# Carried-state products of an mLSTM block: fp32 products on 32 rows, against fp16 halves stacked over 128 partitions by the DMA queue

## The reference

```python
def step(carry, xs):                       # for every token of a sequence
    C, n, m = carry
    q_t, k_t, v_t, i_t, f_t = xs
    f_log = jax.nn.log_sigmoid(f_t)
    m_new = jnp.maximum(f_log + m, i_t)
    F = jnp.exp(f_log + m - m_new)
    I = jnp.exp(i_t - m_new)
    C_new = F[..., None, None] * C + (I[..., None] * k_t)[..., :, None] * v_t[..., None, :]
    n_new = F[..., None] * n + I[..., None] * k_t
    h_num = jnp.einsum('bhd,bhdv->bhv', q_t * scale, C_new)
    qn = jnp.einsum('bhd,bhd->bh', q_t * scale, n_new)
    h = h_num / (jnp.maximum(jnp.abs(qn), jnp.exp(-m_new)) + EPS)[..., None]
...
x = x + (sigmoid(o_preact) * multihead_norm(h)) @ Wout.T
x = x + gelu(layernorm(x) @ w1_q.T + b1) @ w2_q.T + b2
```

## Time and profile before

| | |
|---|---|
| median of 3 runs | 1802.92 us |
| the profiled execution | 1805.18 us |
| its span | 1803.4 us |
| TensorE busy (matmul) | 1755.5 us, 97% |
| VectorE busy | 1373.7 us, 76% |
| ScalarE busy | 1069.4 us, 59% |
| GpSimd busy | 588.0 us, 33% |
| mean granted TensorE clock | 0.983 of 2.4 GHz |

### The profile page before, as it was taken

One profiled execution on the slowest core, in us unless ns is written; L12 is line 12 of the kernel. 1 busy time (PEld: TensorE's weight loads), 2 busy tenths in 40 slices (PEclk: granted clock), 3 DMA queues, 4 the chain that ended last, 5 costly groups with the idle time before them and its releaser, 6 DMA issues.

```text
span 1803.4 us, 31974 instructions
## 1 busy us (share of the span) xinstructions
PE 1755.5 (97%) x12524; PEld 882.3 (49%) x12524; DVE 1373.7 (76%) x2464; ACT 1069.4 (59%) x1801; POOL 588.0 (33%) x481
## 2 busy tenths in 40 slices
PE   5779999999999999999999999999999999999999
PEld 3464544445454444544445454444544444454555
DVE  6777777788777778878777787877778777885772
ACT  5866638375573737547374764737466383756643
POOL 1232342514324251432524143252423325242340
PEclk8859999999999999999999999999999999999999
DMA  8423225151422524142251413325142332414020
GB/s 287 173 83 103 54 69 128 48 150 23 122 54 53 144 48 140 23 127 58 54 144 38 132 41 106 80 54 144 36 114 49 98 100 54 121 25 127 1 53 24
DMA packets 233526, 156.97 MB, mean 87 GB/s; under 512 B 195089, under 2 KB 199313, under 8 KB 228257
## 3 DMA queue, kind: packets, MB, share of 16 engines
q1 hardware_dynamic: 231792, 151.79, 31.0%
q10 hardware_dynamic: 1584, 3.15, 0.5%
HBM read 90.48 MB, written 17.24 MB: 60 GB/s over the span
## 4 chain that ended last, share of the span: by engine, by line
PE 91%; DVE 2%; ACT 1%; issue 1%; POOL 1%; DMA 0%; POOLq 0%; DVEq 0%; ACTq 0%
PE pf L1976 24%; PE pf L1960 23%; PE pa L1819 20%; PE pa L1795 9%; PE psh L1819 6%; PE psh L1916 2%; PE psh L1900 1%; PE psh L1877 1%; PE pa L1786 1%; PE psh L1950 1%; PE psh L1858 1%; PE pa L1916 1%; PE psh L1833 1%; DVE kT L1468 0%; ACT dec L930 0%
## 5 line engine op out<-in xcount | busy, mean ns | idle before, releaser
L1976 PE MATMUL pf<-w2T,gT 128*128 128x512 f16 x2048 | 497.1, 379 | 0.0
L1960 PE MATMUL pf<-x2T,w1T 128*128 128x512 f16 x1920 | 422.1, 380 | 0.0
L1960 PEld LDWEIGHTS pf<-x2T,w1T 128*128 128x128 f16 x1920 | 185.3, 98 | 222.7
L1522 DVE SCALAR_TENSOR_TENSOR gT<-g,wscale,gT 128x512 f16<-128x512 f32 x240 | 212.2, 884 | 105.7 <-ACT gT L966 105.1
L1976 PEld LDWEIGHTS pf<-w2T,gT 128*128 128x128 f16 x2048 | 195.3, 97 | 176.4
L1819 PE MATMUL pa<-wT,xT 128*128 128x512 f16 x960 | 213.6, 380 | 1.0 <-ACT sig L889 0.9
L963 ACT ACTIVATE g<-pf,b1c 128x512 f32<-128x512 f32 x240 | 164.0, 683 | 75.7 <-PE pf L1960 73.5
L971 ACT ACTIVATE ktok<-kT 128x512 f32<-128x512 f32 x64 | 40.4, 631 | 265.0 <-DVE kT L1446 265.0
L1819 PE MATMUL pa<-wT,shared 128*128 128x512 f16 x768 | 177.7, 382 | 0.7 <-DMA shared<-qT 0.6
L966 ACT ACTIVATE gT<-g,wscale 128x512 f16<-128x512 f32 x240 | 173.2, 722 | 7.8
L1795 PE MATMUL pa<-xT,wT 128*128 128x512 f16 x768 | 171.3, 380 | 0.1
(11 more groups left out here) (228 smaller groups left out, 2679.6 us busy)
## 6 DMA issues: line engine op xcount, KB each, us to landing
dec<-gate_r SPq DMA_DIRECT2D x32, 1024.0 KB, 5.6
xin<-L_attn_x SPq DMA_DIRECT2D x16, 1024.0 KB, 6.1
out<-x1b SPq DMA_DIRECT2D x64, 256.0 KB, 2.2
xres<-L_attn_x SPq DMA_DIRECT2D x16, 512.0 KB, 5.9
xres<-L_attn_x SPq DMA_DIRECT2D x32, 256.0 KB, 3.0
qw<-gate_w SPq DMA_DIRECT2D x128, 48.0 KB, 5.7
gT<-L_ffn_w SPq DMA_DIRECT2D x5, 1024.0 KB, 4.8
gT<-L_ffn_w ACTq DMA_DIRECT2D x3, 1024.0 KB, 5.9
```

What stands on the lines that cost most here:

```text
L1522: nc.vector.scalar_tensor_tensor(gT[:, LO, f, :], g32[:, f % 2, :], wscale[:, W_GELU:W_GELU + 1], gT[:, HI, f, :], ALU.mult, ALU.subtract) ...
L1960: last = nc.tensor.matmul(bank, w1T[:, k, tok(f)], x2T[:, part, :, k, :], start=(k == 0 and part == HI), stop=(k == KD - 1 and part == LO))
L1976: last = nc.tensor.matmul(bank, gT[:, part, f, tok(t)], w2T[:, f, :], start=(f == 0 and part == HI), stop=(f == NF - 1 and part == LO), sk ...
```

## The change

The product with the state is taken in f16 halves. The four products of halves, HI HI, HI LO, LO HI and LO LO, are 4 x 32 = 128 rows of one product. VectorE makes the halves of `qw` and `cst` (`split_queries`, `split_states`, two instructions each), SP copies them with 32 small DMAs into stacked form (`stack_states`), and `chunk_head` issues one f16 product of 128 rows in front of each head's three. Sequence 0 stays as it was. The halves lie in `kT` (queries) and `ktok` (states), so `head_stats(b, 0)` on VectorE waits for all 32 DMAs before it writes there. The constants (SCORE_SPLIT, ONES, Q_STACK and the scales made from them) change values only.

```diff
+        s4 = sb("s4", [P, H4, T - 1, HG, VA], F16)
+        q4_first = sb("q4_first", [P, HG, LATE], F16)
...
+        q4 = [q4_first[:, :, :], qw_half[:, 0, :, :], qw_half[:, 1, :, :],
+              xres[:, T - 1, :].bitcast(F16)[:, 0:HG * LATE].rearrange("p (g s) -> p g s", g=HG)]
...
+            def stack_states(b):
+
+                sp.wait_ge(q16_ok, at(b - 1, 1, 1))
+                for i in range(H4):
+                    for r in range(4):
+                        sp.dma_start(q4[i][r * DQ:(r + 1) * DQ, :, :],
+                                     q16[i * DQ:(i + 1) * DQ, r // 2, :, :]).then_inc(q4_loaded, 16)
+                sp.wait_ge(s16_ok, at(b - 1, 1, 1))
+                for i in range(H4):
+                    for r in range(4):
+                        sp.dma_start(s4[r * DQ:(r + 1) * DQ, i, :, :, :].rearrange("p c g v -> p (c g v)"),
+                                     s16[i * DQ:(i + 1) * DQ, r % 2, :]).then_inc(s4_loaded, 16)
...
                 transpose_x(b + 1)
+                stack_states(b)
                 heads_out(b, b - 1)
...
+            def split_queries(b):
+
+                dve.wait_ge(qw_ok, at(b, 1, 1))
+                nc.vector.tensor_scalar(q16[:, HI, :, :], qw[:, :, :], split_scale[:, 2:3], None, ALU.mult).then_inc(q16_hi, 1)
+                dve.wait_ge(q16_hi, at(b - 1, 1, 1))
+                nc.vector.scalar_tensor_tensor(q16[:, LO, :, :], qw[:, :, :], split_scale[:, 2:3], q16[:, HI, :, :],
+                                               ALU.mult, ALU.subtract).then_inc(q16_ok, 1)
+
+            def split_states(b):
+
+                states = cst[:, :, :, :].rearrange("p c g v -> p (c g v)")
+                dve.wait_ge(ph_free, at(b, PH_USES, U_U + 1))
+                nc.vector.tensor_scalar(s16[:, HI, :], states, split_scale[:, 3:4], None, ALU.mult).then_inc(s16_hi, 1)
+                dve.wait_ge(s16_hi, at(b - 1, 1, 1))
+                nc.vector.scalar_tensor_tensor(s16[:, LO, :], states, split_scale[:, 3:4], s16[:, HI, :],
+                                               ALU.mult, ALU.subtract).then_inc(s16_ok, 1)
...
+                if j == 0 and not (isinstance(b, int) and b == 0):
+                    dve.wait_ge(q4_loaded, at(b - 1, 256, 256))
+                    dve.wait_ge(s4_loaded, at(b - 1, 256, 256))
                 den_of = den[:, :].rearrange("p (a h) -> p a h", h=H4)
...
                     hidden(0, 1)
+                    split_queries(b)
...
                         state(b, 2)
+                        if run_f:
+                            split_states(b)
...
-                if j == 1:
+                if j == 1 and not (isinstance(b, int) and b == 0):
+                    pe.wait_ge(q4_loaded, at(b - 1, 256, 256))
+                    pe.wait_ge(s4_loaded, at(b - 1, 256, 256))
+                elif j == 1:
                     pe.wait_ge(qw_ok, at(b, 1, 1))
...
+                    if j > 0:
+                        nc.tensor.matmul(out_cols, q4[i][:, g, tok(j - 1)], s4[:, i, j - 1, g, :], start=(j == 1 and g == 0),
+                                         stop=False, skip_group_check=True)
```

More of the change, by code:

```diff
@@ L39 @@
 V_SPLIT = 2.0 ** -5 / X_SCALE
-SCORE_SPLIT = 2.0 ** -16
+SCORE_SPLIT = 2.0 ** -20
+ONES = 2.0 ** 10
+Q_STACK = 2.0 ** 27
 TINY = 2.0 ** -100
@@ L144, in block_program @@
         gcol = sb("gcol", [P, KD])
-        split_scale, head_scale = sb("split_scale", [P, 2]), sb("head_scale", [P, 3])
+        split_scale, head_scale = sb("split_scale", [P, 4]), sb("head_scale", [P, 3])
         evac = sb("evac", [P, 6])
@@ L186, in block_program @@
         square = head_sum[:, :, 0:DHV]
+        q16 = (kT[:, :, :].bitcast(F16).rearrange("p g s -> p (g s)")[:, 0:2 * HG * LATE]
+               .rearrange("p (a g s) -> p a g s", a=2, g=HG))
+        s16 = (ktok[:, :, :].bitcast(F16).rearrange("p c d -> p (c d)")[:, 0:2 * HG * (T - 1) * VA]
+               .rearrange("p (a n) -> p a n", a=2))
+        qw_half = qw[:, :, :].bitcast(F16).rearrange("p g s -> p (g s)").rearrange("p (i g s) -> p i g s", i=2, g=HG)
+        q4 = [q4_first[:, :, :], qw_half[:, 0, :, :], qw_half[:, 1, :, :],
+              xres[:, T - 1, :].bitcast(F16)[:, 0:HG * LATE].rearrange("p (g s) -> p g s", g=HG)]
         k_halves, q_halves = (hoT[:, :, :, :, :].rearrange("p t a k c -> p (t a k c)")
@@ L261, in block_program @@
         cst_ok = sem("cst_ok")
+        q16_hi, q16_ok, s16_hi, s16_ok = sem("q16_hi"), sem("q16_ok"), sem("s16_hi"), sem("s16_ok")
+        q4_loaded, s4_loaded = sem("q4_loaded"), sem("s4_loaded")
         kq_split = sem("kq_split")
@@ L568, in _ @@
             residual(B - 1, RES_TILES[1])
+            stack_states(B - 1)
             heads_out(B - 1, B - 2)
@@ L587, in _ @@
             nc.gpsimd.memset(half[:, :], -0.5)
-            nc.gpsimd.memset(vaug[:, :, :, DHV:VA], 1.0).then_inc(s_pchain, 1)
+            nc.gpsimd.memset(vaug[:, :, :, DHV:VA], ONES).then_inc(s_pchain, 1)
             pool.wait_ge(s_pchain, 1)
@@ L1152, in scales @@
                     nc.vector.tensor_scalar(gate_bias[:, :], gate_bias[:, :], 1.0 / CAP, None, ALU.mult)
-                    nc.vector.tensor_scalar(head_scale[:, 2:3], wscale[:, W_V:W_V + 1], MLSTM_EPS * 2.0 ** -10,
+                    nc.vector.tensor_scalar(head_scale[:, 2:3], wscale[:, W_V:W_V + 1], MLSTM_EPS * 2.0 ** -10 / ONES ** 2,
                                             wscale[:, W_V:W_V + 1], ALU.mult, ALU.mult)
@@ L1162, in scales @@
                     nc.vector.tensor_scalar(evac[:, W_GELU:W_GELU + 1], to_score, score * DQ ** -0.5 / X_SCALE, None, ALU.mult)
-                    nc.vector.tensor_scalar(head_scale[:, 0:1], to_score, score, to_score, ALU.mult, ALU.mult)
-                    nc.vector.tensor_scalar(head_scale[:, 1:2], to_score, MLSTM_EPS * score, to_score, ALU.mult, ALU.mult)
+                    nc.vector.tensor_scalar(head_scale[:, 0:1], to_score, score * ONES, to_score, ALU.mult, ALU.mult)
+                    nc.vector.tensor_scalar(head_scale[:, 1:2], to_score, MLSTM_EPS * score * ONES, to_score, ALU.mult, ALU.mult)
                     nc.vector.tensor_scalar(evac[:, W_O:W_O + 1], winv[:, W_O:W_O + 1], 1.0 / X_SCALE, None, ALU.mult)
@@ L1169, in scales @@
                     nc.vector.tensor_scalar(split_scale[:, 1:2], qk, 2.0 ** -5 / score, None, ALU.mult)
+                    nc.vector.tensor_scalar(split_scale[:, 2:3], qk, Q_STACK, None, ALU.mult)
+                    nc.vector.tensor_scalar(split_scale[:, 3:4], wscale[:, W_QK:W_QK + 1], 1.0 / Q_STACK, None, ALU.mult)
                     nc.vector.tensor_scalar(gcol[:, :], gcol[:, :], wscale[:, W_OUT:W_OUT + 1], None, ALU.mult).then_inc(s_scales, 1)
```

## The result

The changed kernel takes 1866.99 us (median of 4 runs, 1865.49 to 1869.24), beside 1802.76 us for the kernel before on the same chip. The ratio is 1.0352 (95% interval 1.034 to 1.0364): 64 us slower. The spans of the two profiled executions are 1864.2 and 1803.4 us, 60.8 apart. The forecast was slower, by 19 us, with a range that ended at 1843.

The account below looks back on a forecast made before the run. PE, busy 97% of the span, was taken to bound the kernel. Chunk 3, waiting on VectorE's delayed chain, cost 0.9 us a block and the second scores 0.37: 1.25, 19 us in all, so 1803.4 became 1822, range 1795 to 1843.

Parts of the forecast that it names:

- the 0.84 us of gain: PE's stream per block: 1.60 us of state products removed, less 0.76 for 24 new short products; 12.6 us in all.
- the stall at the scores: PE waits for banks before the second group's scores, since VectorE's query split delays the weighs: 0.37 us a block (0 to 0.8).
- the forecast chain: Late state copies hold VectorE's head_stats(0) from 318.79 to 322.3, so PE's chunk 3 starts at 336.75, not 336.11.
- Their pace: eight loads of 32 partitions take SP 3.67 us, 0.46 each: SP's 16 state copies, issued from 313.9 at 0.46 us each: the last issued at 320.8, landed at 322.2.
- the forecast's own sum: Per block: project(0) 0.9 us later behind VectorE's chain, plus 0.37 at the second scores: 1.25 us, 19 us in all.
- PE at chunk 1 wants them at 322.66 - no loss yet: State copies land at 322.2, before PE's chunk 1 needs them at 322.66, so PE loses nothing there.
- rival C: SBUF-to-SBUF copies land after 5.7 us, like the qw loads: 65 us more, 1887; chance 0.06, shared with anything above 1845.
- The chain's inner lengths: VectorE in head_stats: 6.5 us from start to the copy of chunk 1's sums, then 7.25 to chunk 2's.
- Rival A: Faster, copies come in time, at a pace of 0.33 us: 1796, or 1790 without the wait before the second scores; chance 0.21.

## Why the prediction was half right

**What held.** PE's side: the new products cost 2.71 us for 8 heads against 2.48, 0.029 us each (forecast 0.0315), so the 0.84 us of gain is real; the kernel without copies shows it, less the stall at the scores. The states' halves were ready 1.59 us after the start of `state(2)` (315.09 to 316.68), as forecast (1.6). SP's issues, then VectorE's wait, then VectorE's copy that chunk 3 needs, is the forecast chain, and it set the start of chunk 3 in all 15 blocks.

**The step that failed** is the sentence "Their pace: eight loads of 32 partitions take SP 3.67 us, 0.46 each". That row is a DRAM load. Copies from SBUF to SBUF are issued 0.63 us apart by themselves, and 0.63 to 0.70 here, by the block. From the first issue to the last landing it is 11.6 us on average (11.2 to 12.3), where 8.3 were forecast: about 2.8 us of the difference are fifteen steps of pace, 0.4 the landing of 1.8 instead of 1.4 us. Put into the forecast's own sum: 1.25 + 3.3 more, and 0.1 more until VectorE starts; less 0.13, since the stall at the scores cost 0.24 and not 0.37, and less 0.42, since chunk 3 started 14.03 us after VectorE's first copy, not 14.45. That makes 4.1 us a block, or 61.5 us in 15 blocks, and the spans differ by 60.8. For sequence 2 alone, with 11.8 us and a start of VectorE 0.54 us after the landing, the same sum gives 4.6, and 4.55 were measured.

**What failed with it** is "PE at chunk 1 wants them at 322.66 - no loss yet". With the true pace the copies land behind the time at which PE wants them, and PE waited 2.7 us for them in each block. The prediction had named that as a sign of rival C, and it came without C's landing. It cost nothing on top only because VectorE's chain was longer still: with VectorE's wait taken away, PE's own wait and the clock that fell after it still cost 53 us (1856.17 beside 1803.54). That a wait of PE can cost clock stood nowhere in the prediction.

**The chain's inner lengths** were each off and cancelled in part, which was luck: 5.20 us to chunk 1's copy instead of 6.5, then 8.07 instead of 7.25. In the second, one small instruction took 2.09 us where it takes 0.22 in the next chunk; GpSimd began its 128x1024 subtraction at the time. Both ended together (339.59 and 339.57). In the kernel before, another small instruction of VectorE, at 328.77, took 1.56 us and also ended with GpSimd's subtraction. That the one slowed the other was only read from the traces, not tried.

**The range was too narrow** because its upper end took the landing as uncertain (1.4 to 2.2 us, times one) and the pace only downwards (0.33 to 0.46, times fifteen). Rival C's 65 us stood on top of the forecast's 19, for 1887, and was 20 too high; its mechanism, a landing of 5.7 us, is refuted by the 1.8 of the page. Rival A was near to what a timely landing gives (1796 forecast, 1796.17 measured with the states through DRAM; without the stall 1790 and 1791.85), in part by luck, since it took the stall at 0.37 and not 0.24. No form of copy from SBUF to SBUF that ran had the pace it needs. The page "DMA: Bandwidth & Descriptors" of the Trainium skill, section "Anatomy of one DMA", gave 2.0 us for a DMA's fixed part, on the path through GpSimd; the rows here, issued by SP and with the transfer in them, are 1.8 for SBUF to SBUF and 2.1 for the store of the states. The same page of the Trainium skill, section "Issuing engines are not separate DMA queues", calls the sequencer's time to initiate a DMA usually small beside the DMA. For this burst the trace does not agree: one issue is 0.66 us beside 1.8 to its landing, and the fifteen issues ahead of the last make 10 of the 11.8 us.

## What to carry to other kernels

Many small DMAs cost their number times the issue pace, so count issues before bytes: here 16 copies of 24 KB took 12 us, five DMAs through DRAM 7. When such a burst stands between a producer and a busy engine, find everything that waits for its last landing, also the engine that only wants the source buffer back. With twelve copies that second wait cost 28 us (1829.71 beside 1801.44), out of 33 over the kernel without copies. With sixteen, taking it away gave only 11 us (1866.99 beside 1856.17), since PE's own wait and the slow clock behind it were nearly as long a path. And price a count times an unseen unit with a range on the unit, since the error is multiplied.

## What the runs showed of the hardware

- In a burst, an issue on SP took 0.63 us from SBUF to SBUF, whether a row had 256 or 1536 bytes and whether there were 16 or 128 rows, and 0.46 us with DRAM on one side (780 bytes; 0.50 over six copies of 128 rows).
- A fourth 65-column product behind a 512-column one cost 0.029 us, its weight load nothing that can be seen.
- After a wait of 3.08 us PE was granted 1.2 GHz for the first five long products and their short ones, 1.5 us more than at 2.4 GHz. In the kernel with the halves in their own place this happened in nine blocks of 15, and cost 1.3 to 2.8 us each time. The length of the wait alone doesn't tell: in the changed kernel the clock fell after 2.38 us in sequence 3 and stayed after 2.88 in sequence 2.
